# Two of the four tile turns behind the first layer moved from the matmul engine to a DMA transpose, with the work between the scan steps regrouped

## The chip, the cores and the metric

The kernel runs on one core of a Trainium2 chip. The metric is the device time of one execution in microseconds (us), lower is better. The kernel before takes 925.98 us, the median of 3 runs (925.22 to 927.23). The profile is of another, single execution of 928.0 us, in which the engines' span is 926.3 us.

## What is computed

The input x has 2 sequences of 4096 rows of 512 numbers. A state-space layer is followed by a layer that routes each row to one of 8 experts; both stand behind a normalisation and have a residual. Cut to what matters:

```python
def attn(x):                      # x is normalised
    s = sigmoid(silu(x @ s_w1.T + s_b1) @ s_w2.T + s_b2)
    u = (x @ B_w.T + B_b) * s     # 128 states
    h[t] = h[t-1] @ A.T + u[t]    # over the 4096 steps
    y = h @ C_w.T + C_b + x @ D_w.T + D_b
    return y * sigmoid(x @ g_w.T + g_b)
def ffn(x):                       # x is normalised
    e = argmax(x @ gate_w.T)
    return x + expert_w[e] applied to x
x = x + attn(layernorm(x))
x = x + ffn(layernorm(x))
```

## The kernel before

The rows are worked off in 16 blocks of 512 rows, 256 of each sequence; a block has 4 tiles of 128 rows. All programs are written out by hand, one per engine, and each engine takes its instructions in the order written. Matmuls are done three times over in a split form (high and low part of each operand), which is why every product stands as L1382, L1383 and L1384 in a row.

In the turn of block b the matmul engine (PE, `body` at L1543) does, in this order: the state part of y of the block before (`y_state`), the two halves of the gating network s1 (L1568, L1572), the input product B into the bank "scan", and then a long stretch in which the scan of block b runs as a chain of nine small steps (`to_pairs`, `to_chunks`, `over` 0 to 5, `to_middles`; `down` gives its result back). Each step is two or three small matmuls, and VectorE (DVE) then adds them to the state z and splits it anew (L970, L972, L962, L964) before the next step can start. Between the steps PE has other work: 48 matmuls of the gate product (`gates`, bank G) and 48 of the dense product (`y_dense`, banks y0 to y3), and the tail of block b - 1.

That tail chooses the experts. When GpSimd (POOL, L569 and L572) has made the tiles of x1, the output of the first layer, PE turns each tile (`tail_turn`, four 128x128 transposes, L1466) into a PSUM bank (tiles 0 and 2 into "turned", tiles 1 and 3 into y3). ScalarE (ACT) copies it out as the high part (`tail_hi`, L680), DVE makes the low part (`tail_lo`, L1023), and eight small products per pair of tiles (`score_product`, L1482 and L1484) give the scores. `tail_back` turns the scores back (L1498) after ACT has copied them (`scoresT`, L686), DVE chooses, and `tail_ranks` counts. The eight products of the first pair stand between the eight transposes of tiles 2 and 3.

The next block's input comes another way: ACT normalises a tile (L695), splits its words into 16-bit halves (`halve`, L704), the queue of SyncE (SP) starts a DMA transpose (`flip`, L356), ACT joins the halves (`join`, L731) and copies the high part (`high`, L738), and DVE makes the low part (`low`, L1167). There are two buffers of halves, of flipped and of joined tiles. The same way is gone by one or two pieces of expert weights per block (L711, L718, L723; `halve_piece`, `join_piece`; L1155 and L1160 on DVE). `high` of tile 3 stands at the head of ACT's next body, and PE's s1 product waits for it (`xT_hi`) at the head of a block. After the 16 blocks a last phase, from about 670 us, applies the experts to the sorted rows.

## Time and profile before

| | |
|---|---|
| median of 3 runs | 925.98 us (925.22 to 927.23) |
| the profiled execution | 928.0 us, span 926.3 us |
| PE matmul busy | 904.1 us, 98% |
| PE weight load busy | 739.5 us, 80% |
| DVE busy | 704.2 us, 76% |
| ACT busy | 597.2 us, 64% |
| POOL busy | 389.8 us, 42% |
| granted clock of PE | 0.996 of full speed |

Matmuls overlap in the pipeline, so a matmul's own duration is longer than its share of the time: what counts is the distance from one start to the next. An idle time stands at an instruction with the one that released it.

### The profile page before, as it was taken

How to read it: one execution, taken by the hardware profiler on the slowest of the kernel's cores; microseconds unless marked ns; L12 is line 12 of the kernel's file. 1: busy time of each engine (PE TensorE's matmuls, PEld its weight loads, DVE VectorE, ACT ScalarE, POOL GpSimd, SP SyncE). 2: the span in 40 equal slices, each digit the busy share in tenths (PEclk: the TensorE clock that was granted, in tenths of full speed). 3: DMA queues.
4: the chain of work that ended last, by engine and by line, in shares of the span. 5: the costliest groups of instructions: out<-in, count | busy, mean ns of one | idle time of the engine just before them, and what ended most of it. 6: DMA issues, size and time to landing. Idle time of an engine off the chain costs nothing.

```text
span 926.3 us, 15829 instructions
## 1 busy us (share of the span) xinstructions
PE 904.1 (98%) x4565; PEld 739.5 (80%) x4566; DVE 704.2 (76%) x1725; ACT 597.2 (64%) x826; POOL 389.8 (42%) x492
## 2 busy tenths in 40 slices
PE   8999999999999999999999999999999999999995
PEld 7777888888888888888888888888868887888884
DVE  6778979788888979788888979788787465555552
ACT  5568676857767675867767685857534345666661
POOL 1032536181634536181634527181623453333432
PEclk9999999999999999999999999999999999999998
DMA  8435384746657474748557485846789868999881
GB/s 311 131 91 140 89 206 114 205 108 171 151 140 187 89 198 120 204 111 171 153 137 186 90 199 118 206 113 178 254 275 413 336 234 243 224 218 219 192 187 39
DMA packets 203593, 165.55 MB, mean 179 GB/s; under 512 B 128245, under 2 KB 161781, under 8 KB 202496
## 3 DMA queue, kind: packets, MB, share of 16 engines
q1 hardware_dynamic: 192576, 130.89, 55.6%
q0 software_dynamic: 10800, 33.70, 10.7%
q8 instruction: 36, 0.59, 0.3%
q14 instruction: 37, 0.30, 0.1%
q10 hardware_dynamic: 144, 0.07, 0.0%
HBM read 81.63 MB, written 54.68 MB: 147 GB/s over the span
## 4 chain that ended last, share of the span: by engine, by line
PE 88%; DVE 3%; issue 2%; SPq 1%; ACT 1%; DMA 1%; POOL 0%; ACTq 0%; DVEq 0%; POOLq 0%
PE y L1662 19%; PE y L1382 7%; PE y L1383 7%; PE y L1384 7%; PE gates L1382 7%; PE gates L1384 6%; PE gates L1383 6%; PE scan L1527 3%; PE turned L1568 3%; PE gates L1568 3%; PE scan L1382 2%; PE scan L1383 2%; PE scan L1384 2%; PE turned L1650 2%; PE scores L1484 2%
## 5 line engine op out<-in xcount | busy, mean ns | idle before, releaser
L1662 PE MATMUL y<-experts,x1T_hi 128*128 x568 | 180.7, 399 | 2.6 <-issue 2.5
L578 POOL TENSOR_SCALAR ln_var_eps<-ln_mean_var 128x4 f32<-128x4 f32 x16 | 3.6, 224 | 302.3 <-DVE ln_mean_var L1017 302.2
L1662 PEld LDWEIGHTS y<-experts,x1T_hi 128*128 128x128 f32 x568 | 103.4, 188 | 24.1 <-issue 4.2
L623 POOL DMA_INDIRECT out<-gate,ids x71 | 72.0, 1015 | 111.1 <-DVE gate L1347 68.2
L1662 PE MATMUL y<-experts,x1T_lo 128*128 x284 | 111.4, 392 | 0.0
L1347 DVE TENSOR_TENSOR gate<-y,raw_weights 128x512 f32<-128x512 f32 x71 | 49.1, 691 | 75.6 <-PE y L1662 50.4
L1382 PE MATMUL gates<-GwT_hi,xT_hi 128*128 128x512 f32 x256 | 104.6, 409 | 0.0
L1382 PE MATMUL y<-DwT_hi,xT_hi 128*128 128x512 f32 x256 | 101.8, 398 | 0.5 <-DVE gateT L939 0.5
L731 ACT ACTIVATE joined<-flipped 128x1024 uint16<-128x1024 uint16 x60 | 82.3, 1371 | 29.7 <-DVE xT_lo L1167 21.1
L1383 PE MATMUL y<-DwT_lo,xT_hi 128*128 128x512 f32 x256 | 100.3, 392 | 0.0
L1384 PE MATMUL y<-DwT_hi,xT_lo 128*128 128x512 f32 x256 | 100.3, 392 | 0.0
L1384 PE MATMUL gates<-GwT_hi,xT_lo 128*128 128x512 f32 x256 | 100.2, 392 | 0.0
L1383 PE MATMUL gates<-GwT_lo,xT_hi 128*128 128x512 f32 x256 | 100.2, 391 | 0.0
L572 POOL TENSOR_TENSOR x_rows<-x_rows,y_biased 128x512 f32<-128x512 f32 x60 | 91.4, 1523 | 4.7
L569 POOL TENSOR_TENSOR y_biased<-y_biased,gate 128x512 f32<-128x512 f32 x60 | 79.4, 1323 | 25.5 <-DVE y_biased L1007 25.5
L970 DVE TENSOR_TENSOR z<-scan,z 128x126 f32<-128x126 f32 (+6 forms) x128 | 35.9, 280 | 54.7 <-PE scan L1527 51.1
L594 POOL DMA_INDIRECT routed_rows<-x_rows,dest x64 | 64.3, 1004 | 24.3 <-issue 23.5
L829 ACT ACTIVATE x1T_hi<-turned 128x512 fp32r<-128x512 f32 x36 | 21.6, 599 | 70.8 <-PE turned L1650 66.5
L704 ACT ACTIVATE halves<-x_in 128x1024 uint16<-128x1024 uint16 x60 | 63.5, 1058 | 1.9
L695 ACT ACTIVATE x_in<-x_in,ln_shift,ln_rstd 128x512 f32<-128x512 f32 x60 | 48.3, 805 | 22.7 <-POOL ln_shift L562 22.7
L1662 PEld LDWEIGHTS y<-experts,x1T_lo 128*128 128x128 f32 x284 | 53.3, 188 | 11.8
L1384 PEld LDWEIGHTS gates<-GwT_hi,xT_lo 128*128 128x128 f32 x256 | 48.0, 188 | 11.1
(276 smaller groups left out, 2340.9 us busy)
## 6 DMA issues: line engine op xcount, KB each, us to landing
raw_weights<-routed_rows SPq DMA_DIRECT2D x71, 258.0 KB
x_in<-L_attn_x SPq DMA_DIRECT2D x32, 512.0 KB, 5.0
x_rows<-L_attn_x SPq DMA_DIRECT2D x32, 512.0 KB, 4.9
turned_experts<-raw_weights SPq DMA_DIRECT2D x32, 512.0 KB, 5.3
experts<-turned_experts SPq DMA_DIRECT2D x8, 2048.0 KB
raw_weights<-L_ffn_expert_w SPq DMA_DIRECT2D x32, 256.0 KB, 3.1
routed_rows<-padrow SPq DMA_DIRECT2D x9, 258.0 KB
out<-gate,ids POOLq DMA_INDIRECT x71
```

The costliest lines, as they stand in the source:

```text
L569: nc.gpsimd.tensor_tensor(yb[:, i, :], yb[:, i, :], gate[:, i, :], ALU.mult).then_inc(S_["gated"], 1)
L572: nc.gpsimd.tensor_tensor(xrow[q][:, i, 0:D], xrow[q][:, i, 0:D], yb[:, i, :], ALU.add).then_inc(S_["x1_ready"], 1)
L594: nc.gpsimd.indirect_dma_start(out=routed, out_offset=bass.IndirectOffsetOnAxis(ap=dest[q][:, i:i + 1], axis=0), in_=xrow[q][:, i, :], in_ ...
L623: nc.gpsimd.indirect_dma_start(out=out_rows, out_offset=bass.IndirectOffsetOnAxis(ap=ids[r][:, 0:1], axis=0), in_=res[r], in_offset=None, ...
L704: nc.scalar.activation(halves[n % 2][:].rearrange("p (h d) -> p h d", h=2), planes(xin[:, i, :]), ACT.Copy).then_inc(S_["x_halves"], 1)
L731: nc.scalar.activation(planes(joined[n % 2][:].rearrange("p k t -> p (k t)")), flipped[n % 2][:].rearrange("p (h k) t -> p h (k t)", h=2), ...
L1347: nc.vector.tensor_tensor(res[r], Y[m % 2][:], rows[m][:, 0:D], ALU.add).then_inc(S_["slot_result"], 1)
L1382: nc.tensor.matmul(dst, left[0], right[0], start=first, stop=False)
L1383: nc.tensor.matmul(dst, left[0], right[1], start=False, stop=False)
L1384: return nc.tensor.matmul(dst, left[1], right[0], start=False, stop=last)
L1568: nc.tensor.matmul((TP, G)[m][:], h[:, k, m * P:(m + 1) * P], xT[0][:, k, :], start=(k == 0 and h is s1T[0]), stop=False)
L1662: ins = nc.tensor.matmul(Y[m % 2][:], x2T[a][:, k, m % 2 * P:(m % 2 + 1) * P], flat[:, bass.ds(first + (w * KD + k) * D, D)], start=(k == ...
```

## The change

For tiles 2 and 3 of x1 of blocks 1 to 13, that is in the turns of blocks 2 to 14, PE's transposes are left out. ACT splits the tile into halves (`halve_x1`), SP starts a DMA transpose, ACT joins the halves (`join_x1`), and `tail_hi` and `tail_lo` read the joined tile in SBUF instead of a PSUM bank. The buffers are the four tiles of y_biased, which are free once x1 is made. In these 13 turns the order is changed too: on PE the products of the first pair stand alone, `gates` of tiles 1 and 2, `y_dense` of tile 3 and the second pair's products are regrouped, and the second `tail_back` goes behind `y_dense` of tile 3; on DVE `tail_lo`, `gate_sum(1)`, `low(b + 1, 0)`, `low_piece`, `add_identity` and `ln2_stats(3)` change places; on ACT `join(b + 1, 2)` goes behind the copies of the state. In all turns from block 1 on, ACT's gate of the old tile 3 goes behind the first sigmoid of s1.

```diff
+        def by_dma(b, i):
+
+            return 0 < b < LASTB - 1 and i >= NT // 2
+
+        def x1_on_pe(b, i):
+
+            return NT * min(b, 1) + NT // 2 * max(0, min(b, LASTB - 1) - 1) + NT * max(0, b - LASTB + 1) + i + 1
+
+        x1_halves = [yb[:, j, :].bitcast(u16) for j in range(2)]
+        x1_flipped = [yb[:, 2 + j, :].bitcast(u16).rearrange("p (c t) -> p c t", t=P) for j in range(2)]
+        x1_joined = [yb[:, j, :] for j in range(2)]
 
...
+                if by_dma(b - 1, NT - 1):
+                    for j in range(2):
+                        sp.wait_ge(S_["x1_halves"], 2 * (b - 2) + j + 1)
+                        sp.dma_start_transpose(x1_flipped[j], x1_halves[j]).then_inc(x1_turned[j], 16)
...
-                act.wait_ge(S_["x2T_psum"], NT * b + i + 1)
-
-                nc.scalar.activation(turned_rows(b, i)[0][:, :, i % 2 * P:(i % 2 + 1) * P], by_block(turn_bank(b, i)), ACT.Copy
+                if by_dma(b, i):
+                    act.wait_ge(S_["x1_joined"], 2 * (b - 1) + i - 1)
+                    src = x1_joined[i - 2].rearrange("p (k t) -> p k t", k=KD)
+                else:
+                    act.wait_ge(S_["x2T_psum"], x1_on_pe(b, i))
+                    src = by_block(turn_bank(b, i))
+                nc.scalar.activation(turned_rows(b, i)[0][:, :, i % 2 * P:(i % 2 + 1) * P], src, ACT.Copy
                                      ).then_inc(S_["x2T_hi"], 1)
+
+            def halve_x1(b, i):
+
+                act.wait_ge(S_["x1_ready"], NT * b + i + 1)
+                nc.scalar.activation(x1_halves[i - 2].rearrange("p (h d) -> p h d", h=2), planes(xrow[b % 2][:, i, 0:D]), ACT.Copy
+                                     ).then_inc(S_["x1_halves"], 1)
+
+            def join_x1(b, i):
+
+                act.wait_ge(x1_turned[i - 2], 16 * b)
+                nc.scalar.activation(planes(x1_joined[i - 2]), x1_flipped[i - 2].rearrange("p (h k) t -> p h (k t)", h=2), ACT.Copy
+                                     ).then_inc(S_["x1_joined"], 1)
 
             def scoresT(b, pair):
...
                 ahead = b < LASTB
+                dma = by_dma(b - 1, NT - 1)
                 if tail:
                     high(b, NT - 1)
-                    gates(b - 1, NT - 1)
...
+                    if tail and m == 0:
+                        gates(b - 1, NT - 1)
...
                     halve_piece(1, 1)
+                if dma:
+                    halve_x1(b - 1, 2)
+                    halve_x1(b - 1, 3)
                 if ahead:
                     halve(b + 1, 0)
                     halve(b + 1, 1)
                 else:
                     join_piece(b, 0)
                     join_piece(b, 1)
-                if tail:
+                if tail and not dma:
                     tail_hi(b - 1, 2)
                     tail_hi(b - 1, 3)
+                if tail:
                     scoresT(b - 1, 0)
-                    if ahead:
-                        join_piece(b, 0)
+                if dma:
+                    for i in range(2, NT):
+                        join_x1(b - 1, i)
+                        tail_hi(b - 1, i)
+                if tail and ahead:
+                    join_piece(b, 0)
...
-                    join(b + 1, 2)
+                    if not dma:
+                        join(b + 1, 2)
                 act.wait_ge(S_["scan_lo"], NSTEP * (b + 1))
...
                 if ahead:
+                    if dma:
+                        join(b + 1, 2)
                     high(b + 1, 2)
                     join(b + 1, 3)
...
-                nc.vector.tensor_tensor(lo, by_block(turn_bank(b, i)), hi.bitcast(f32), ALU.subtract
+                src = x1_joined[i - 2].rearrange("p (k t) -> p k t", k=KD) if by_dma(b, i) else by_block(turn_bank(b, i))
+                nc.vector.tensor_tensor(lo, src, hi.bitcast(f32), ALU.subtract
...
                 over(b, 0)
-                if tail:
+                if dma:
+                    ln2_stats(old, oldq, 3)
+                elif tail:
                     tail_lo(old, 2)
                 over(b, 1)
                 gate_sum(b, 0)
+                if dma:
+                    for j in range(2):
+                        add_identity(b + 1, j)
                 if not ahead:
                     list_tiles(0)
                 over(b, 2)
-                if tail:
+                if dma:
+                    tail_lo(old, 2)
+                elif tail:
                     tail_lo(old, 3)
-                if tail and ahead:
+                if tail and ahead and not dma:
                     for j in range(2):
                         add_identity(b + 1, j)
                 over(b, 3)
-                gate_sum(b, 1)
+                if not dma:
+                    gate_sum(b, 1)
                 over(b, 4)
-                if tail and ahead:
+                if dma:
+                    gate_sum(b, 1)
+                if tail and ahead and not dma:
                     low_piece(b, 0)
                 if not ahead:
                     list_gaps()
                     slot_experts(0, FIRST)
                 over(b, 5)
-                if ahead:
+                if dma:
+                    tail_lo(old, 3)
+                elif ahead:
                     low(b + 1, 0)
                 else:
                     slot_rows(0, FIRST)
                 to_middles(b)
+                if dma:
+                    low(b + 1, 0)
                 gate_sum(b, 2)
...
                     place(old, oldq, oldturn)
-                    ln2_stats(old, oldq, 3)
+                    if dma:
+                        low_piece(b, 0)
+                    else:
+                        ln2_stats(old, oldq, 3)
...
-                        wait(pe, S_["x2T_lo"], NT * b)
+                        wait(pe, S_["x2T_lo"], NT * (b - 1) + 2 if by_dma(b - 1, NT - 1) else NT * b)
...
                 to_chunks(b)
-                if tail:
+                if tail and not by_dma(b - 1, 2):
                     tail_turn(b - 1, 1 - q, 2, True)
+                elif tail:
+                    for n in range(KD):
+                        score_product(b - 1, 0, n)
                 gates(b, 0, 1, 2)
                 over(b, 0)
-                if tail:
+                if tail and not by_dma(b - 1, 3):
                     tail_turn(b - 1, 1 - q, 3, True)
+                elif tail:
+                    for n in range(KD, 2 * KD):
+                        score_product(b - 1, 0, n)
                 gates(b, 0, 3)
                 y_dense(b, 2, 0)
                 over(b, 1)
@@ -1615,22 +1686,38 @@
                 gates(b, 1, 0, 1)
                 if tail:
                     tail_back(b - 1, 0)
-                gates(b, 1, 2)
-                over(b, 3)
-                gates(b, 1, 3)
-                if tail:
+                if not by_dma(b - 1, NT - 1):
+                    gates(b, 1, 2)
+                    over(b, 3)
+                    gates(b, 1, 3)
+                    if tail:
+                        tail_scores(b - 1, 1)
+                    over(b, 4)
+                    y_dense(b, 3, 0, 1)
+                    if tail:
+                        tail_back(b - 1, 1)
+                    over(b, 5)
+                    gates(b, 2, 0, 1)
+                    to_middles(b)
+                    gates(b, 2, 2, 3)
+                    y_dense(b, 3, 2)
+                    down(b)
+                    y_dense(b, 3, 3)
+                else:
+                    over(b, 3)
+                    gates(b, 1, 2, 3)
+                    over(b, 4)
+                    y_dense(b, 3, 0, 1)
+                    over(b, 5)
+                    y_dense(b, 3, 2)
+                    gates(b, 2, 0)
+                    to_middles(b)
+                    gates(b, 2, 1)
                     tail_scores(b - 1, 1)
-                over(b, 4)
-                y_dense(b, 3, 0, 1)
-                if tail:
+                    gates(b, 2, 2, 3)
+                    down(b)
+                    y_dense(b, 3, 3)
                     tail_back(b - 1, 1)
-                over(b, 5)
-                gates(b, 2, 0, 1)
-                to_middles(b)
-                gates(b, 2, 2, 3)
-                y_dense(b, 3, 2)
-                down(b)
-                y_dense(b, 3, 3)
```

PE behind the step `to_chunks` in the turn of a middle block, before ("turned" is the bank, x_rows the tile of x1, x1T the turned tile, gateT the router's weights):

```order
L1527 MATMUL scan<-chunk_ends,A_powers_hi 128x256 [waits scan_lo]
L1527 MATMUL scan<-chunk_ends,A_powers_lo 128x256
L1466 MATMUL turned<-ident,x_rows 128x128 [waits x2T_lo,x1_ready]
L1484 MATMUL scores<-x1T_hi,gateT 16x256 [waits x2T_lo]
L1466 MATMUL turned<-ident,x_rows 128x128
L1484 MATMUL scores<-x1T_hi,gateT 16x256
L1466 MATMUL turned<-ident,x_rows 128x128
L1484 MATMUL scores<-x1T_hi,gateT 16x256
L1466 MATMUL turned<-ident,x_rows 128x128
L1482 MATMUL scores<-x1T_lo,gateT 8x256
L1382 MATMUL gates<-GwT_hi,xT_hi 128x512
```

and now:

```order
L1592 MATMUL scan<-chunk_ends,A_powers_hi 128x256 [waits scan_lo]
L1592 MATMUL scan<-chunk_ends,A_powers_lo 128x256
L1549 MATMUL scores<-x1T_hi,gateT 16x256 [waits x2T_lo]
L1549 MATMUL scores<-x1T_hi,gateT 16x256 x2
L1547 MATMUL scores<-x1T_lo,gateT 8x256
L1447 MATMUL gates<-GwT_hi,xT_hi 128x512
L1448 MATMUL gates<-GwT_lo,xT_hi 128x512
```

The four transposes (L1466) are gone and four score products remain between the step and the gate product; behind the next step the same holds for the other four.

ACT in the middle of a block's turn, behind the two `tail_hi` of tiles 0 and 1, before (in_ x_in is the next block's input; x1T_late is the turned tile 2 or 3; raw_weights is a piece of expert weights):

```order
L695 ACTIVATE x_in<-x_in,ln1_shift,ln1_rstd 128x512 [waits shift1_ready]
L704 ACTIVATE halves0<-x_in 128x1024 [waits x_turned_even,xn_ready]
L695 ACTIVATE x_in<-x_in,ln1_shift,ln1_rstd 128x512 [waits shift1_ready]
L704 ACTIVATE halves1<-x_in 128x1024 [waits x_turned_odd,xn_ready]
L680 ACTIVATE x1T_late_hi<-turned 128x4x128 [waits x2T_psum]
L680 ACTIVATE x1T_late_hi<-y3 128x4x128 [waits x2T_psum]
L686 ACTIVATE scoresT<-scores 16x256 [waits scoresT_psum]
L718 ACTIVATE raw_weights<-raw_weights 128x2x512 [waits expert_low0,expert_flip0]
L723 ACTIVATE raw_weights<-raw_weights 128x512 [waits expert_sent0,expert_joined0]
```

and now (y_biased holds the halves, the flipped and the joined tile of x1):

```order
L707 ACTIVATE y_biased<-x1_rows1 128x1024 [waits x1_ready] x2
L728 ACTIVATE x_in<-x_in,ln1_shift,ln1_rstd 128x512 [waits shift1_ready]
L737 ACTIVATE halves0<-x_in 128x1024 [waits x_turned_even,xn_ready]
L728 ACTIVATE x_in<-x_in,ln1_shift,ln1_rstd 128x512 [waits shift1_ready]
L737 ACTIVATE halves1<-x_in 128x1024 [waits x_turned_odd,xn_ready]
L719 ACTIVATE scoresT<-scores 16x256 [waits scoresT_psum]
L713 ACTIVATE y_biased<-y_biased 128x2x512 [waits x1_turned_third]
L701 ACTIVATE x1T_late_hi<-y_biased 128x4x128 [waits x1_joined]
L713 ACTIVATE y_biased<-y_biased 128x2x512 [waits x1_turned_fourth]
L701 ACTIVATE x1T_late_hi<-y_biased 128x4x128 [waits x1_joined]
L751 ACTIVATE raw_weights<-raw_weights 128x2x512 [waits expert_low0,expert_flip0]
L756 ACTIVATE raw_weights<-raw_weights 128x512 [waits expert_sent0,expert_joined0]
```

Two `halve_x1` (the row with x2) stand ahead of the next block's input, two `join_x1` (L713) behind the first copy of the scores.

ACT from the second copy of the scores to the end of a turn, before:

```order
L686 ACTIVATE scoresT<-scores 16x256 [waits scoresT_psum]
L690 ACTIVATE gate<-gate 128x512 [waits g_sum]
L738 ACTIVATE xT_hi<-joined1 128x4x128 [waits g_psum,joined]
L695 ACTIVATE x_in<-x_in,ln1_shift,ln1_rstd 128x512 [waits shift1_ready]
L704 ACTIVATE halves1<-x_in 128x1024 [waits x_turned_odd,xn_ready]
L731 ACTIVATE joined0<-flipped0 128x2x512 [waits xT_lo,x_turned_even]
L810 ACTIVATE hT_hi<-z_half_hi 128x128x2 [waits scan_lo]
L810 ACTIVATE hT_lo<-z_half_lo 128x128x2
L690 ACTIVATE gate<-gate 128x512 [waits g_sum]
L814 ACTIVATE hT_hi<-z 128x128x2 [waits h_sum]
L738 ACTIVATE xT_hi<-joined0 128x4x128 [waits g_psum,joined]
L731 ACTIVATE joined1<-flipped1 128x2x512 [waits xT_lo,x_turned_odd]
L738 ACTIVATE xT_hi<-joined1 128x4x128 [waits g_psum,joined]
```

and now:

```order
L719 ACTIVATE scoresT<-scores 16x256 [waits scoresT_psum]
L723 ACTIVATE gate<-gate 128x512 [waits g_sum]
L771 ACTIVATE xT_hi<-joined1 128x4x128 [waits g_psum,joined]
L728 ACTIVATE x_in<-x_in,ln1_shift,ln1_rstd 128x512 [waits shift1_ready]
L737 ACTIVATE halves1<-x_in 128x1024 [waits x_turned_odd,xn_ready]
L854 ACTIVATE hT_hi<-z_half_hi 128x128x2 [waits scan_lo]
L854 ACTIVATE hT_lo<-z_half_lo 128x128x2
L723 ACTIVATE gate<-gate 128x512 [waits g_sum]
L858 ACTIVATE hT_hi<-z 128x128x2 [waits h_sum]
L764 ACTIVATE joined0<-flipped0 128x2x512 [waits xT_lo,x_turned_even]
L771 ACTIVATE xT_hi<-joined0 128x4x128 [waits g_psum,joined]
L764 ACTIVATE joined1<-flipped1 128x2x512 [waits xT_lo,x_turned_odd]
L771 ACTIVATE xT_hi<-joined1 128x4x128 [waits g_psum,joined]
```

The join of the next block's tile 2 (joined0) went from ahead of the state's copies (hT) to behind them; the rest is as it was.

## Rows read from the trace of the kernel before

**Rows 1.** The page: busy time, share of the span and instructions of each engine

```profile
PE 904.1 (98%) x4565; PEld 739.5 (80%) x4566; DVE 704.2 (76%) x1725; ACT 597.2 (64%) x826; POOL 389.8 (42%) x492
```

**Rows 2.** Timeline of PE's weight loads: `tail_ranks` of the first and last of eight blocks

```profile
350.13 0.10 PEld L1506 LDWEIGHTS scores<-onehot,strictly_before 128*128 128x128 bf16 x1 [0.26 <-issue]
...
641.59 0.10 PEld L1506 LDWEIGHTS scores<-onehot,strictly_before 128*128 128x128 bf16 x1 [0.26 <-issue]
```

**Rows 3.** Timeline of PE, tile 2 turned: start, us, engine, line, operation

```profile
329.06 0.28 PE L1527 MATMUL scan<-chunk_ends,A_powers_hi 128*128 128x256 f32 x1
...
329.30 0.27 PE L1466 MATMUL turned<-ident,x_rows 128*128 128x128 f32 x1
...
330.21 0.39 PE L1382 MATMUL gates<-GwT_hi,xT_hi 128*128 128x512 f32 x1
```

**Rows 4.** Timeline of PE, a scan step, three gate products, the second pair's scores

```profile
339.15 0.27 PE L1527 MATMUL scan<-chunk_ends,A_powers_hi 128*128 128x224 f32 x1
...
340.06 0.51 PE L1484 MATMUL scores<-x1T_late_hi,gateT 128*16 128x256 f32 x3
...
340.99 0.25 PE L1527 MATMUL scan<-chunk_ends,A_powers_hi 128*128 128x192 f32 x1
```

**Rows 5.** Timeline of DVE, the scan steps that these two starts release

```profile
339.57 0.28 DVE L970 TENSOR_TENSOR z<-scan,z 128x112 f32<-128x112 f32 x1 [0.53 <-PE scan L1527]
...
340.45 0.28 DVE L964 TENSOR_TENSOR chunk_ends<-z,chunk_ends 128x112 fp32r<-128x112 f32 x1
...
341.39 0.27 DVE L970 TENSOR_TENSOR z<-scan,z 128x96 f32<-128x96 f32 x1
```

**Rows 6.** Timeline of DVE and PE: a step that waited for its split

```profile
326.04 0.42 DVE L964 TENSOR_TENSOR z_half_lo<-z,z_half_hi 128x256 fp32r<-128x256 f32 x1
...
326.64 0.29 PE L1382 MATMUL scan<-z_half_hi,A_powers_hi 128*128 128x256 f32 x1
```

**Rows 7.** Timeline of PE around the first `tail_back`

```profile
337.80 0.40 PE L1384 MATMUL gates<-GwT_hi,xT_lo 128*128 128x512 f32 x1
...
338.68 0.40 PE L1383 MATMUL gates<-GwT_lo,xT_hi 128*128 128x512 f32 x1
```

**Rows 8.** Timeline of PE, `down`, the state product and s1 behind it

```profile
347.03 0.28 PE L1382 MATMUL scan<-z_half_hi,A_powers_hi 128*128 128x256 f32 x1
...
351.05 0.39 PE L1382 MATMUL y<-CwT_hi,hT_hi 128*128 128x512 f32 x1
...
353.84 0.39 PE L1568 MATMUL turned<-xT_hi,s1T_hi 128*128 128x512 f32 x1
```

**Rows 9.** Timeline of ACT from the second copy of the scores to the block's end

```profile
342.35 0.35 ACT L686 ACTIVATE scoresT<-scores 16x256 f32<-16x256 f32 x1
...
344.47 1.06 ACT L704 ACTIVATE halves<-x_in 128x1024 uint16<-128x1024 uint16 x1
...
348.11 0.44 ACT L814 ACTIVATE hT_hi<-z 128x256 fp32r<-128x256 f32 x1 [0.20 <-DVE z L1258]
348.45 0.62 ACT L738 ACTIVATE xT_hi<-joined 128x512 fp32r<-128x512 f32 x1
350.36 1.38 ACT L731 ACTIVATE joined<-flipped 128x1024 uint16<-128x1024 uint16 x1 [1.29 <-DVE xT_lo L1167]
351.77 0.63 ACT L738 ACTIVATE xT_hi<-joined 128x512 fp32r<-128x512 f32 x1
```

**Rows 10.** Timeline of ACT, the same block's middle

```profile
325.50 0.59 ACT L680 ACTIVATE x1T_hi<-y 128x512 fp32r<-128x512 f32 x1
327.60 0.82 ACT L695 ACTIVATE x_in<-x_in,ln_shift,ln_rstd 128x512 f32<-128x512 f32 x1 [1.51 <-POOL ln_shift L562]
...
334.38 0.60 ACT L680 ACTIVATE x1T_late_hi<-y 128x512 fp32r<-128x512 f32 x1 [2.58 <-remote]
```

**Rows 11.** DMAs issued in 345 to 346.5 us: count, median us to landing

```profile
flipped<-halves SPq DMA_TRANSPOSE x1, 3.1
```

**Rows 12.** DMAs issued in 331 to 332 us

```profile
flipped<-halves SPq DMA_TRANSPOSE x1, 5.4
```

4 lines of the change are left out of this document (3 added, 1 removed).

## The prediction

> **What bounds the kernel now.** I read the page's busy times first: PE is busy 98% of the span, DVE 76%, ACT 64%, POOL 42% [rows 1]. Then the timeline of PE's weight loads, for the pace: the same instruction comes at 350.13 and seven blocks later at 641.59 [rows 2], so a block takes 291.46 / 7 = 41.64 us. Last the timelines of PE, DVE and ACT in one block: s1 of block b starts at 312.12 and s1 of block b + 1 at 353.84 [rows 8]; all clock times below are of this block. PE has no long wait in it. But a busy PE is not the only bound: it keeps pace with two chains that come close to it, the scan (PE, DVE, PE) and, at the block's end, ACT's way to the next block's input (`join`, `high`), without which s1 can't start. The change takes work from PE and gives work to ACT, so the question is which of these chains is late next.
>
> **What goes from PE.** Four transposes with four score products between them take 330.21 - 329.30 = 0.91 us [rows 3]; there are two such groups, 1.82 us. Eight score products alone take 340.99 - 340.06 = 0.93 us [rows 4]. So PE loses 0.89 us per block, in 13 blocks 11.6 us. All other products of PE are the same in number; only their places change.
>
> **What the regrouping costs in the scan.** A step is two products, 0.24 us, and a gate or dense product takes (340.06 - 339.15 - 0.23) / 3 = 0.228 us [rows 3, 4]. DVE starts 0.42 us after PE's step and needs 1.16 us for its four instructions (339.57 to 340.73) [rows 4, 5]; PE's next step can start 0.18 us after the end of the split (326.46 to 326.64) [rows 6]. The loop is thus 1.76 us, with slightly narrower data 1.70 and 1.65 (the last two estimated). PE's work between the steps is now: behind `to_chunks` and `over` 0, 0.24 + 0.47 + 6 x 0.228 = 2.07 us; behind `over` 1, 2.28; behind `over` 2, 2.01 with a `tail_back`, which costs 338.68 - 337.80 - 2 x 0.228 = 0.42 us [rows 7]; behind `over` 3, 4 and 5 only 0.22 + 1.37 = 1.59 us. There the loop is longer, and PE waits 0.17 + 0.11 + 0.06 = 0.34 us per block. Another DVE instruction between two steps adds nothing: from the end of a split to the next step's first addition 0.66 us pass with a gate sum between (340.73 to 341.39) [rows 5], and without one the loop itself needs 0.18 + 0.42 = 0.60.
>
> From 329.06 (`to_chunks`) on, PE's steps are then: `over` 0 at 331.13, 1 at 333.20, 2 at 335.49, 3 at 337.50, 4 at 339.26, 5 at 340.96, `to_middles` at 342.61. Behind that stand three gate products and the eight of the second pair, whose last one starts at 344.35 and ends 0.3 us later. `down` is at 342.61 + 0.24 + 0.68 + 0.93 + 1.37 = 345.83. From `down` to the state product it was 4.02 us, now 0.42 more for the second `tail_back`: 350.27. From there to s1 it is 2.79 as before [rows 8]: PE would be ready at 353.06, 0.78 before the 353.84 of now.
>
> **What ACT gets.** Two `halve_x1` have the form of the halves instruction (1.06 us, 0.97 from start to start), two `join_x1` that of the join (1.41 us to the start of the `high` that waits for it) [rows 9]. Nothing in the trace shows them with these operands; as the shapes and the memory are the same I bound each between 0.9 and 1.5 us. The first two fall into ACT's idle time: tail_hi ends at 326.09 and the next instruction waited until 327.60 [rows 10]. ACT is 0.35 late behind them (327.95). From 327.60 to the second copy of the scores at 342.35 it had 14.75 - 2.58 = 12.17 us of work [rows 9, 10]. With two joins (2.8) and some 0.4 of waiting for the first scores it comes to the second copy at 343.3. But the second pair's products now end only at 344.65, so it stands there until S = 344.7. That is where this ACT chain is fixed, with 1.4 us of slack ahead of it. The new DMA transposes have their own time hidden: issued at 327.1 and 328.4, wanted at 332.4 and 334.3. The shortest flip lands in 3.1 us [rows 11], one amid other traffic in 5.4 [rows 12]; at 5.4 both still come in time, and what is lost above it is first taken from the 1.4 us. SP's queue has each of its further flips issued later by at most the 1.3 us of two issues, and the tiles are wanted 6 us later. `tail_lo` of the last tile is wanted by PE at 343.5 and DVE makes it behind `over` 5, at 343.0: free, if narrowly.
>
> From the second copy of the scores on ACT has one serial chain: gate, high, normalise, halve, state copies, gate, state copy, join of tile 2 (moved in order, same sum), high, join of tile 3, high. Before it ran from 342.35 to 352.40, with 0.20 and 1.29 idle: 8.56 us of work [rows 9]. Now it starts at S: the last `high` ends at 344.7 + 8.56 = 353.26. s1's weight load and first product follow 0.18 later [rows 6]: 353.44. PE was ready at 353.06 and waits 0.38 us. So **ACT's chain sets the block's end**, and `gates` of the old tile 3, put behind the first sigmoid, takes idle time of ACT there and nothing else: zero.
>
> The flip of the next block's tile 3 lies inside this chain: its halves end at S + (345.53 - 342.35) = 347.88, and its join is reached at S + 8.56 - 0.63 - 1.41 = 351.22. A flip of 3.1 us lands at 351.0. The cover is only 0.2 us.
>
> **The sum.** The block takes 353.44 - 312.12 = 41.32 us against 41.64: 0.32 less, in 13 blocks 4.2 us. The profiled execution takes 928.0 us (span 926.3), so 923.8 by the sum; its time is 2.0 above the median of the runs, so I predict 925.98 - 4.2 = **921.8 us**. The last phase and blocks 0, 1 and 15 keep their time. The uncertain terms are the durations of ACT's new instructions (0.9 to 1.5 us each, in front of 1.4 us of slack: nothing, or at the long end nothing still, 4 x 0.3 = 1.2) and S itself, on which each 0.1 us is 1.3 us in all.
>
> **The rivals.** *PE keeps the bound.* If ACT's chain runs a little shorter than from the rows (0.38 us of 8.56), s1 starts at 353.06 and the block takes 40.94: 0.70 x 13 = 9.1 us, 916.9 us. If the scan waits vanish as well it is 0.89 x 13 = 11.6 us, 914.4. For it: PE is 98% busy and waits for nobody now. Against it: the chain consists of instructions whose durations vary by hundredths, and ACT starts it 2.3 us later than before. [...]
>
> *The chain eats the gain.* If S comes 0.2 to 0.4 later than worked out (PE's wait in each scan step by 0.1 longer, as with POOL's traffic beside DVE), or the chain itself is 0.3 longer, the block takes 41.6: 0 +- 0.14 x 13, 926 us.
>
> *The last flip is late: slower.* If the flip of the next tile 3 takes longer than 3.1 us, join, high and s1 all move by it. It may take 3.3; at 3.6 the gain of 0.32 is gone, and each tenth above costs 1.3 us. Half way between the two flips seen, 4.25 us, the block takes 42.28: 13 x 0.64 = 8.3 us slower, 934.3 us; at 5.4, 23 us. For it: the two added transposes push the traffic of the block's middle back, and one flip amid traffic took 5.4 [rows 12]. Against it: this flip, issued at 345.5, took 3.1 [rows 11], and nothing stands directly ahead of it in SP's queue now that did not before. The Trainium skill ("DMA: Bandwidth & Descriptors", section "Issuing engines are not separate DMA queues") says that DMAs of SP and POOL run on the same 16 engines and interleave. By that rule POOL's scatters, not only SP's queue, delay the new transposes; rows 12 agree, and it speaks for this rival.
>
> That the change doesn't do what it says is excluded by the order of the instructions: the transposes are gone from PE in 13 turns.
>
> **The numbers.** A difference below 0.2% (1.85 us) can't be told from none. ACT's chain as worked out, gain 1.9 to 6.5 us: 0.47. PE keeps the bound, 7 us and more: 0.18. The chain eats it, within 1.85 us: 0.18. The late flip or another thing on ACT, slower: 0.17. Faster 0.65, same 0.18, slower 0.17. The range that leaves out 2 in 10 goes from 915.5, above the full PE saving, to 928.5; the forecast's own is 919.5 to 924.1.
>
> **What would show it.** Right: a block of about 41.3 us in 13 blocks; before s1 PE waits some 0.4 us for `xT_hi`; ACT waits 1 us or more at the second copy of the scores and no longer for `xT_lo` ahead of the join of tile 3; waits of 0.1 to 0.2 us of PE behind `over` 3 to 5. Wrong: ACT arrives at the second copy later than the scores (new instructions too long, or the x1 flips late), ACT waits for a DMA at `join`, or PE waits at the state product for h_lo or at `tail_back`, which I count as covered by 0.2 us or more.

## The result, and the profile after

The changed kernel takes 931.6 us (931.1 to 932.5, 4 runs) against 926.0 us of the kernel before on the same chip (925.2 to 927.2): ratio 1.0061 [1.0046, 1.0076]. It is slower by 5.6 us, where the forecast had 4.2 us less. The profiled execution has a span of 930.7 us against 926.3.

The page of the kernel after, busy times, answers to [rows 1]:

```profile
PE 905.8 (97%) x4461; PEld 722.3 (78%) x4462; DVE 713.4 (77%) x1725; ACT 653.3 (70%) x878; POOL 388.2 (42%) x492
```

PE has 104 matmuls fewer and is no less busy. A busy time isn't work alone: the end of a matmul is modelled, and the first product of s1, which waited, counts 0.47 us where the ones behind it count 0.39. ACT has gained 56 us. The pace, from the timeline of the weight loads of `tail_ranks` (now L1571), answers to [rows 2]:

```profile
182.40 0.10 PEld L1571 LDWEIGHTS scores<-onehot,strictly_before 128*128 128x128 bf16 x1 [0.27 <-issue]
...
308.69 0.10 PEld L1571 LDWEIGHTS scores<-onehot,strictly_before 128*128 128x128 bf16 x1 [0.27 <-issue]
```

Three blocks take 126.29 us, so one takes 42.10 (before 41.64, forecast 41.32). The first changed block takes 41.01, the next twelve 42.1 each, but for one of 43.05. In that one ACT waits 1.13 us for the next block's first flip, which was issued at 331.94 and landed 9.8 us later.

PE at the head of a block and at the end of its scan leg; this answers to [rows 8] (s1) and [rows 6] (the first scan step):

```profile
270.56 0.47 PE L1633 MATMUL turned<-xT_hi,s1T_hi 128*128 128x512 f32 x1
...
285.86 0.39 PE L1447 MATMUL scan<-z_half_hi,A_powers_hi 128*128 128x256 f32 x1 [0.24 <-DVE z_half_lo L1010]
...
303.64 0.28 PE L1549 MATMUL scores<-x1T_late_hi,gateT 128*16 128x256 f32 x1
```

From s1 to the first scan step it is now 285.86 - 270.56 = 15.30 us; before it was 326.64 - 312.12 = 14.52. PE waits for VectorE there. From that step to the last score product it is 17.78 us.

ACT's timeline behind it, with the wait at the second copy of the scores, answers to [rows 9]:

```profile
303.95 0.37 ACT L719 ACTIVATE scoresT<-scores 16x256 f32<-16x256 f32 x1 [1.10 <-PE scores L1549]
304.24 0.61 ACT L723 ACTIVATE gate<-gate 128x512 f32<-128x512 f32 x1
...
306.11 1.06 ACT L737 ACTIVATE halves<-x_in 128x1024 uint16<-128x1024 uint16 x1
...
310.46 1.37 ACT L764 ACTIVATE joined<-flipped 128x1024 uint16<-128x1024 uint16 x1
311.86 0.63 ACT L771 ACTIVATE xT_hi<-joined 128x512 fp32r<-128x512 f32 x1
```

The chain has no gap: 303.95 to 312.49 is 8.54 us, forecast 8.56. VectorE's next `low` of tile 3 starts at 312.53, PE's s1 at 312.64.

VectorE from one `low` of tile 3 to the end of z_half_lo, kernel after:

```profile
270.45 0.69 DVE L1214 TENSOR_TENSOR xT_lo<-joined,xT_hi 128x512 fp32r<-128x512 f32 x1 [0.23 <-ACT xT_hi L771]
...
274.65 0.73 DVE L1176 SCALAR_TENSOR_TENSOR silu<-turned,s_b_col,silu 128x512 f32<-128x512 f32 x1
...
276.08 1.79 DVE L1171 TENSOR_TENSOR siluT_lo<-silu,siluT_hi 128x512 fp32r<-128x512 f32 x1
277.80 0.74 DVE L1176 SCALAR_TENSOR_TENSOR silu<-gates,s_b_col,silu 128x512 f32<-128x512 f32 x1
...
279.24 1.72 DVE L1171 TENSOR_TENSOR siluT_lo<-silu,siluT_hi 128x512 fp32r<-128x512 f32 x1
280.88 1.27 DVE L1057 BATCH_NORM_STATS2 ln_stats<-x_rows 128x6 f32<-128x512 f32 x2
...
282.35 1.68 DVE L1207 TENSOR_TENSOR raw_weights<-raw_weights 128x512 fp32r<-128x512 f32 x1
283.96 0.86 DVE L1185 SCALAR_TENSOR_TENSOR z<-scan,B_b_col,select 128x256 f32<-128x256 f32 x2
...
285.38 0.43 DVE L1010 TENSOR_TENSOR z_half_lo<-z,z_half_hi 128x256 fp32r<-128x256 f32 x1
```

The same stretch in the kernel before (it ends with [rows 6]):

```profile
311.34 0.68 DVE L1167 TENSOR_TENSOR xT_lo<-joined,xT_hi 128x512 fp32r<-128x512 f32 x1
...
315.77 0.75 DVE L1129 SCALAR_TENSOR_TENSOR silu<-turned,s_b_col,silu 128x512 f32<-128x512 f32 x1 [0.16 <-ACT silu L759]
...
317.22 1.05 DVE L1124 TENSOR_TENSOR siluT_lo<-silu,siluT_hi 128x512 fp32r<-128x512 f32 x1
318.49 0.75 DVE L1129 SCALAR_TENSOR_TENSOR silu<-gates,s_b_col,silu 128x512 f32<-128x512 f32 x1 [0.21 <-ACT silu L759]
...
319.94 1.30 DVE L1124 TENSOR_TENSOR siluT_lo<-silu,siluT_hi 128x512 fp32r<-128x512 f32 x1
321.16 1.27 DVE L1011 BATCH_NORM_STATS2 ln_stats<-x_rows 128x6 f32<-128x512 f32 x2
...
322.63 1.56 DVE L1160 TENSOR_TENSOR raw_weights<-raw_weights 128x512 fp32r<-128x512 f32 x1
324.61 0.88 DVE L1138 SCALAR_TENSOR_TENSOR z<-scan,B_b_col,select 128x256 f32<-128x256 f32 x2 [0.41 <-ACT select L775]
```

Three things are to be seen. Before, `low` of tile 3 starts 0.78 us ahead of s1; after, only 0.11, because both wait for ACT's last `high`. Before, VectorE waits for ACT in three places (0.16, 0.21, 0.41); after, it waits nowhere behind `low`, it is the late one. And the two siluT_lo have grown from 1.05 and 1.30 to 1.79 and 1.72 us. From the start of `low` to the end of z_half_lo the stretch is 15.12 us before and 15.36 after. Counted from each start to the next, the two siluT_lo add 0.45 and 0.42, the distances ahead of the first silu and behind the raw_weights row give 0.23 and 0.37 back, the rest 0.03. The way from s1 to the first scan step is then 0.67 (head start lost) + 0.24 - 0.13 = 0.78 us longer. The 0.13 is how the rows count: PE's step stands 0.05 behind z_half_lo instead of 0.18, but that product then takes 0.10 us longer.

The reason why siluT_lo grew can be read from POOL's timeline of the kernel after:

```profile
276.03 1.29 POOL L589 TENSOR_TENSOR x_rows<-x_rows,y_biased 128x512 f32<-128x512 f32 x1
277.27 1.76 POOL L586 TENSOR_TENSOR y_biased<-y_biased,gate 128x512 f32<-128x512 f32 x1
279.11 1.30 POOL L589 TENSOR_TENSOR x_rows<-x_rows,y_biased 128x512 f32<-128x512 f32 x1
280.37 1.75 POOL L586 TENSOR_TENSOR y_biased<-y_biased,gate 128x512 f32<-128x512 f32 x1
282.19 1.29 POOL L589 TENSOR_TENSOR x_rows<-x_rows,y_biased 128x512 f32<-128x512 f32 x1
```

siluT_lo starts at 276.08, just behind the start of a POOL addition that ends at 277.32, and ends at 277.87, 0.55 later. The second siluT_lo and the raw_weights row, a subtraction too, end 0.55 behind the POOL additions that end at 280.41 and 283.48. Before, siluT_lo met POOL in another phase:

```profile
316.42 1.31 POOL L569 TENSOR_TENSOR y_biased<-y_biased,gate 128x512 f32<-128x512 f32 x1
317.80 1.63 POOL L572 TENSOR_TENSOR x_rows<-x_rows,y_biased 128x512 f32<-128x512 f32 x1
```

The first of these ended at 317.73 and siluT_lo at 318.27, 0.54 behind it, but it had begun 0.8 us before siluT_lo. So these VectorE subtractions, with both inputs in SBUF, wait for the 128x512 GpSimd instruction that is in progress. The Trainium skill ("SBUF — State Buffer", section "SBUF: two separate sides") says that the two engines share a port pair as an exclusive lock, held for the whole instruction. These rows agree. One other row doesn't: `low` at 270.45 (0.69 us, two inputs in SBUF too) kept its usual length beside a 128x4 instruction of POOL that lasted from 270.12 to 271.16, so that small instruction didn't hold it up.

### The profile page after: what moved, and what is told of

It is laid out like the page before. It is cut to its first block, busy times and chain, and to the rows that moved or that the text cites. A ratio compares the mean times of both kernels' runs of the same rounds, so it can differ in the third digit from the quotient of the medians.

```text
span 930.7 us, 15673 instructions
## 1 busy us (share of the span) xinstructions
PE 905.8 (97%) x4461; PEld 722.3 (78%) x4462; DVE 713.4 (77%) x1725; ACT 653.3 (70%) x878; POOL 388.2 (42%) x492
## 4 chain that ended last, share of the span: by engine, by line
PE 58%; DVE 15%; ACT 11%; issue 7%; DMA 2%; SPq 2%; DVEq 0%; POOL 0%; ACTq 0%; POOLq 0%
PE y L1749 19%; PE gates L1447 4%; PE y L1447 4%; PE y L1449 4%; PE y L1448 4%; PE gates L1449 4%; PE gates L1448 4%; ACT joined L764 3%; PE scan L1592 3%; DVE y_biased L1053 3%; DVE siluT_lo L1171 2%; DVE ln_stats L958 2%; DVE silu L1176 2%; PE turned L1737 2%; ACT siluT_hi L799 2%
## 5 line engine op out<-in xcount | busy, mean ns | idle before, releaser
L586 POOL TENSOR_TENSOR y_biased<-y_biased,gate 128x512 f32<-128x512 f32 x60 | 90.1, 1501 | 25.5 <-DVE y_biased L1053 25.5
L589 POOL TENSOR_TENSOR x_rows<-x_rows,y_biased 128x512 f32<-128x512 f32 x60 | 79.5, 1325 | 4.7
L1449 PEld LDWEIGHTS y<-DwT_hi,xT_lo 128*128 128x128 f32 x256 | 48.0, 188 | 10.4
```

What stands on the lines that cost most here:

```text
L586: nc.gpsimd.tensor_tensor(yb[:, i, :], yb[:, i, :], gate[:, i, :], ALU.mult).then_inc(S_["gated"], 1)
L589: nc.gpsimd.tensor_tensor(xrow[q][:, i, 0:D], xrow[q][:, i, 0:D], yb[:, i, :], ALU.add).then_inc(S_["x1_ready"], 1)
L1449: return nc.tensor.matmul(dst, left[1], right[0], start=False, stop=last)
```

## The loop

A block of the kernel after, link by link: VectorE's stretch (270.45 to 285.81) 15.36, to PE's step 0.05, PE's scan leg to the last score product 17.78, to ACT's copy 0.31, ACT's chain 8.54, to the next `low` 0.04. The sum is 42.08, and the pace is 42.10. So VectorE's head stretch, PE's scan leg and ACT's tail chain follow each other in a ring, and the kernel is bound by the sum of three parts on three engines.

The first changed block is a test by itself, since the block ahead of it is still of the old form and leaves VectorE its head start (0.79 us):

```profile
102.17 0.68 DVE L1214 TENSOR_TENSOR xT_lo<-joined,xT_hi 128x512 fp32r<-128x512 f32 x1
...
108.06 1.02 DVE L1171 TENSOR_TENSOR siluT_lo<-silu,siluT_hi 128x512 fp32r<-128x512 f32 x1
```
```profile
102.96 0.39 PE L1633 MATMUL turned<-xT_hi,s1T_hi 128*128 128x512 f32 x1
...
144.20 0.47 PE L1633 MATMUL turned<-xT_hi,s1T_hi 128*128 128x512 f32 x1
```

Here siluT_lo takes 1.02 us, the first scan step comes 14.50 us behind s1, and s1 of the next block 41.24 us behind: the block that the forecast worked out (41.32). From the second changed block on `low` is only some 0.12 us ahead, the first siluT_lo takes 1.8 us, and the block 42.1.

The theory LOOP of the experiments is this ring; a microsecond taken from any part of it should show in every block, until PE's own work (40.94 us) is the longest. The experiments limit this for the first part, VectorE's, in which POOL has a say. The rivals are the DMA transposes (DMA), PE's regrouped scan leg by itself (SCAN) and, for VectorE's part, contention with POOL (PORT).

## Experiments

Each time stands beside the kernel before on the same chip (925.9 to 926.4 us). "Block" is the pace of the weight loads of `tail_ranks`.

**Two statistics taken out of VectorE's stretch.** In the changed blocks `ln2_stats(old, oldq, 0)` and `(…, 1)` go from VectorE's head stretch to behind `over` 3 and `to_middles`.

```diff
-                if tail:
+                if tail and not dma:
                     ln2_stats(old, oldq, 0)
                     ln2_stats(old, oldq, 1)
...
+                if dma:
+                    ln2_stats(old, oldq, 0)
...
                 if dma:
                     low(b + 1, 0)
+                    ln2_stats(old, oldq, 1)
```

> The changed kernel, with two of VectorE's statistics of x1 (ln2_stats 0 and 1, 0.6 us each from start to start) taken out of its stretch at the head of a block and put behind over 3 and to_middles, where VectorE waits 0.56 and 1.00 us. Theory LOOP: a block's length is the loop of VectorE's unbroken stretch from low(3) to the first split (15.36 us), the scan up to the second pair's scores (18.1) and ACT's chain to the last high (8.5), 42.1 in all. 1.2 us less in the first leg brings PE's own bound back: about 41.3 us a block, 13 x 0.76 = 9.9 us less than the changed kernel, 922 us. Theory DMA (ACT is late because the added transposes come late): no change, 931 to 932 us. Theory SCAN (the closer scan steps cost it): no change or slower, 931 to 933 us.

Measured: 926.4 us (923.5 to 928.6, 10 runs), ratio 1.0008 [0.9996, 1.0021]; block 41.6. The direction is LOOP's, and 5 us came back, fewer than expected. VectorE's timeline says why:

```profile
269.06 0.69 DVE L1214 TENSOR_TENSOR xT_lo<-joined,xT_hi 128x512 fp32r<-128x512 f32 x1 [0.23 <-ACT xT_hi L771]
...
274.69 1.79 DVE L1171 TENSOR_TENSOR siluT_lo<-silu,siluT_hi 128x512 fp32r<-128x512 f32 x1
...
282.03 0.88 DVE L1185 SCALAR_TENSOR_TENSOR z<-scan,B_b_col,select 128x256 f32<-128x256 f32 x2 [0.77 <-ACT select L810]
```

siluT_lo still meets POOL in the bad phase, and since s2 on PE waits for it, VectorE now waits 0.77 us for `select`. The stretch fell by 0.53 us to 14.83.

**ACT's chain shortened.** `halve(b + 1, 3)` (normalise and split, 1.86 us) goes ahead of the second copy of the scores, into the time in which ACT waited anyway.

```diff
+                if dma:
+                    halve(b + 1, 3)
                 if tail:
                     scoresT(b - 1, 1)
                 gates(b, 1)
                 if ahead:
                     high(b + 1, 1)
-                    halve(b + 1, 3)
+                    if not dma:
+                        halve(b + 1, 3)
```

> The changed kernel, with ACT's halve of the next block's tile 3 (normalise and halves, 1.80 us) ahead of the second copy of the scores, where ACT waits 1.14 us. Theory LOOP: ACT's leg falls by 1.1 us, a block to about 41.0 to 41.3, 917 to 921 us. Theory DMA: ACT is late at the second copy in any case, so the halve only changes places: 930 to 932 us. Theory SCAN: no change, 931 to 932 us.

Measured: 917.5 us (915.9 to 918.9), ratio 0.9907 [0.9884, 0.9929]; block 40.95 (one of 41.57). LOOP holds, and this version beats both kernels. VectorE and PE of it:

```profile
225.42 0.68 DVE L1217 TENSOR_TENSOR xT_lo<-joined,xT_hi 128x512 fp32r<-128x512 f32 x1
...
231.29 1.05 DVE L1174 TENSOR_TENSOR siluT_lo<-silu,siluT_hi 128x512 fp32r<-128x512 f32 x1
...
234.01 1.30 DVE L1174 TENSOR_TENSOR siluT_lo<-silu,siluT_hi 128x512 fp32r<-128x512 f32 x1
...
238.68 0.88 DVE L1188 SCALAR_TENSOR_TENSOR z<-scan,B_b_col,select 128x256 f32<-128x256 f32 x2 [0.42 <-ACT select L810]
```
```profile
240.70 0.29 PE L1450 MATMUL scan<-z_half_hi,A_powers_hi 128*128 128x256 f32 x1
```

`low` has its head start back, siluT_lo its 1.05 and 1.30, and from s1 (226.19) to the first scan step it is 14.51 us as before. In the one block of 41.57 `low` is only 0.44 ahead, siluT_lo takes 1.80 and 1.73 us again, and the step comes 14.97 us behind s1: the head start and the two siluT_lo change together. The other blocks take the 40.94 that the prediction gave for the rival "PE keeps the bound".

**Both.** The two edits together.

> Both edits together (statistics later, halve early). Theory LOOP: the loop is about 39.8 us and PE's own work sets the block, 40.9 to 41.1 us: 916 to 919 us, the best of all. Theories DMA and SCAN: 930 to 932 us.

Measured: 917.6 us (917.0 to 918.2), ratio 0.9909 [0.9891, 0.9927]; block 40.95. The first edit is worth 5 us while the ring binds and nothing once PE does.

**The new order alone.** All turns of x1 stay on PE; PE's new order is kept, VectorE's where it can be. Of ACT's, one part is lost, which the text put on record before the run doesn't say: `join(b + 1, 2)` depends on the same condition and stands ahead of the state copies again. The opposite, the DMA turns in PE's old order, wasn't tried: there PE wants tile 3's low part ahead of `over` 4, and VectorE makes it behind `over` 5.

```diff
         def by_dma(b, i):
-            return 0 < b < LASTB - 1 and i >= NT // 2
+            return False
...
-                if not by_dma(b - 1, NT - 1):
+                if not regrouped(b - 1):
                     gates(b, 1, 2)
```

> The new order of PE (gate, dense and score products regrouped between the scan steps, second tail_back at the end) and of VectorE as far as it can be kept, but tiles 2 and 3 turned on PE as before: no added DMA transpose and no added work on ACT. Theory LOOP: the reordering costs PE's waits behind over 3 to 5, 0.3 to 0.4 us a block, and ACT's chain has room: about 42.0 us a block, 929 to 931 us. Theory DMA: without the transposes nothing is late, as before: 926 us. Theory SCAN: all of the loss and the 0.89 us that the turns give back: 42.1 + 0.9 us a block, 940 us or more.

Measured: 955.7 us (955.3 to 956.1), ratio 1.0319 [1.0301, 1.0337]; block 43.9. That is far above the 929 to 931 us of LOOP, and of the three numbers only SCAN's "940 us or more" holds. The order costs much, and the changed kernel, with the DMA turns and the `join` moved, has most of it back. DMA as the main cause is refuted, above all by the second experiment, in which the transposes stand and the time is 917.5 us. SCAN is refuted there too, since it expected no change from ACT's move. ACT and PE:

```profile
312.15 0.37 ACT L723 ACTIVATE scoresT<-scores 16x256 f32<-16x256 f32 x1 [4.62 <-PE scores L1548]
```
```profile
318.63 0.48 PE L1446 MATMUL y<-CwT_hi,hT_hi 128*128 128x512 f32 x1 [0.68 <-DVE hT_lo L1325]
```

ACT stands 4.6 us until PE's late score products, with its whole tail chain behind it. PE then waits 0.68 us at the state product for hT_lo, the low part of the state. From the second copy of the scores (312.15) to the next s1 (321.51) 9.36 us pass, in the changed kernel 8.69. The 0.67 us are the price of the `join` at its old place, as the experiment on it below shows, in 13 blocks 8.7 of the 30 us.

**The same with ACT's chain shortened.** The edit of the second experiment on top of the order alone.

> The new order of PE and ACT with all turns of x1 kept on PE (that kernel alone took 955.7 us, 43.9 a block, with ACT standing 4.6 us at the second copy of the scores), and halve(b + 1, 3) moved ahead of the second copy of the scores. Theory (the block is a loop through ACT's chain behind the second copy of the scores): the chain gets shorter by the two halves, 1.8 to 2.1 us, as when the same move was made in the changed kernel, where it shortened the stretch from s1 to pairs as well: block 41.8 to 42.2, 928 to 933. Rival (PE's own scan leg with the turns in it sets the pace, and ACT's wait is only its slack): no change, 43.9, 954 to 957.

Measured: 936.4 us (935.8 to 938.4), ratio 1.0114 [1.0094, 1.0135]; block 42.4. The rival (no change) is refuted: 19 of the 30 us came back by ACT's move alone. The time is 3 us above what was expected. The `join` is at its old place here too, but PE no longer waits for hT_lo. s1 now follows PE's state products without a wait (313.45, then 314.15), so ACT is out of the ring and PE's own leg, with some waits for VectorE, sets the pace (three weight loads of scan steps stand idle 0.16 to 0.29 us for it). Against the second experiment, which differs in the turns, VectorE's order and the `join`, it is 42.40 - 40.95 = 1.45 us a block, more than the 0.89 that the transposes cost.

**`join` of tile 2 put back ahead of the state copies.**

```diff
                 if ahead:
                     high(b + 1, 1)
                     halve(b + 1, 3)
-                    if not dma:
-                        join(b + 1, 2)
+                    join(b + 1, 2)
```

> The changed kernel with ACT's join of the next block's tile 2 put back ahead of the copies of the state. Theory LOOP: ACT's chain keeps its sum, but hT and with it h_lo come 1.24 us later; PE waits for h_lo at the state product some 0.8 us, and s1 and the whole loop move by about 0.6: 42.7 us a block, 938 to 940 us. Rival, that only the sum of ACT's chain counts: 931 to 932 us.

Measured: 937.7 us (937.2 to 938.4), ratio 1.0127 [1.0110, 1.0145]; block 42.44. That part of the change was worth 6 us. PE shows the price of the old place:

```profile
312.01 0.48 PE L1444 MATMUL y<-CwT_hi,hT_hi 128*128 128x512 f32 x1 [0.69 <-DVE hT_lo L1322]
```

This is the path that was expected: ACT's copies of the state come later, with them hT_lo, and PE waits 0.69 us for it at the state product, in all 13 blocks. From the second copy of the scores (305.53) to s1 (314.89) 9.36 us pass instead of 8.69. Half of it comes back at the block's head, where the first scan step stands 14.96 us behind s1 instead of 15.30. The last join waits too, 0.64 us for VectorE's `low` of the tile before, but ACT's last `high` behind it ends 0.28 us ahead of s1, so that wait isn't the one that ends last.

**`gates` of the old tile 3 put back** to the head of ACT's body.

```diff
                     high(b, NT - 1)
+                    gates(b - 1, NT - 1)
...
-                    if tail and m == 0:
-                        gates(b - 1, NT - 1)
```

> The changed kernel with one edit undone: gates of the old tile 3 stand at the head of ACT's body again, ahead of the first sigmoid. The prediction priced that edit at zero, because ACT has idle time there. Loop theory (a block is VectorE's stretch from low(3) to z_half_lo, 15.4 us, then the scan leg, 17.7 us, then ACT's chain from the second copy of the scores, 8.5 us): the gates are in none of the three, since ACT is waiting for the scores 1.1 us at the end of the scan leg. Block 42.1 us, 931 to 932.5. Rival (gates delay ACT's select or its copies at the block's head, and VectorE waits for them): 0.3 us or more per block, 936 or more when put back, or 928 or less if it was the new place that hurt.

Measured: 932.9 us (931.4 to 933.3), ratio 1.0065 [1.0046, 1.0084]; block 42.1. The block is the same, as the prediction priced it.

**One statistic more in VectorE's stretch.** `ln2_stats(old, oldq, 2)` goes from behind `to_pairs` into the stretch, in the changed kernel and in the kernel before.

```diff
                     ln2_stats(old, oldq, 1)
+                    ln2_stats(old, oldq, 2)
...
                 to_pairs(b)
-                if tail:
-                    ln2_stats(old, oldq, 2)
```

> The changed kernel with a third statistic of x1 (ln2_stats 2, 0.6 us) moved from behind to_pairs into VectorE's stretch at the head of a block. Theory LOOP: VectorE has no idle time there, so each block gets its full length more, 0.6 us, in 13 blocks 7.8 us: 939 us. Rival DMA: no change, 931 to 932 us.

> The same edit on the kernel before. There VectorE has about 0.9 us of idle time in that stretch, 0.41 of it right ahead of the first split. Theory LOOP: most of the 0.6 us is absorbed, at most 0.2 us a block reach PE: 926 to 929 us, clearly less than the 7.8 us on the changed kernel. Rival (the instruction costs its length wherever it stands): 926 + 15 x 0.6 = 935 us.

Measured: changed kernel 931.9 us (931.4 to 935.0), ratio 1.0070 [1.0044, 1.0096], block 42.10, so nothing: a miss. Kernel before 927.9 us (925.6 to 931.4, 10 runs), ratio 1.0018 [1.0002, 1.0034], block 41.61, as expected; the 2 us more don't stand in the blocks. VectorE in the changed kernel with this edit:

```profile
283.00 1.87 DVE L1057 BATCH_NORM_STATS2 ln_stats<-x_rows 128x6 f32<-128x512 f32 x3
...
285.07 1.08 DVE L1207 TENSOR_TENSOR raw_weights<-raw_weights 128x512 fp32r<-128x512 f32 x1
...
287.50 0.43 DVE L1010 TENSOR_TENSOR z_half_lo<-z,z_half_hi 128x256 fp32r<-128x256 f32 x1
```

The 0.6 us more of work came out of the wait of the raw_weights row, 1.08 instead of 1.68. The stretch isn't a sum of VectorE's own work: it ends 2.32 us behind POOL's last addition (285.61 to 287.93), and in the changed kernel it is 2.33 (283.48 to 285.81).

**POOL started earlier.** `ln2_mv(old)`, which releases POOL, goes ahead of `choose` on VectorE.

```diff
+                if dma:
+                    ln2_mv(old)
                 if tail:
                     choose(old)
...
-                if tail:
+                if tail and not dma:
                     ln2_mv(old)
```

> The changed kernel with ln2_mv of the old tile moved ahead of choose on VectorE, so that POOL's rstd2 and its residual additions behind it can start earlier; VectorE's own sum of work in the stretch stays the same. Theory A (the stretch low(3) to z_half_lo ends by POOL's additions, behind each of which a two-operand instruction of VectorE ends 0.55 us later): the residual starts 0.28 us earlier (on its data instead of on rstd2), the stretch falls from 15.36 to about 15.1 or less, the block to 41.8 or less, 928 or less; if the two-operand instructions fall into another phase of POOL's, as in the kernel before (1.05 and 1.30 us instead of 1.79 and 1.72), down to 41.1, 921. Theory B (VectorE's stretch is a plain sum of its own instructions): same sum, 42.1, 931 to 932.5.

Measured: 930.7 us (929.9 to 932.9), ratio 1.0049 [1.0032, 1.0066]; block 42.0. The stretch is 15.26 us (271.03 to 286.29) and ends again 2.33 us behind POOL's last addition (283.96). POOL gained only 0.11 us against `low`, because its first product then waits for VectorE's y_biased. So theory A missed with its numbers (a block of 41.8 or less, 928 us or less), and the times can't tell 1 us from none. What speaks for it is the trace alone, the same 2.33 us behind POOL.

**POOL's product cut to an eighth.** POOL multiplies only 64 of 512 columns by the gate; the rest stays without it, so rows go to other experts.

```diff
-                    nc.gpsimd.tensor_tensor(yb[:, i, :], yb[:, i, :], gate[:, i, :], ALU.mult
+                    nc.gpsimd.tensor_tensor(yb[:, i, 0:64], yb[:, i, 0:64], gate[:, i, 0:64], ALU.mult
```

> The changed kernel with seven eighths of GpSimd's product y * gate left out (64 of 512 columns are multiplied), so that GpSimd is at work some 5 us less per block while VectorE makes siluT_lo. Theory PORT, as part of LOOP (siluT_lo takes 1.79 and 1.72 us in the changed kernel against 1.05 and 1.30 before, because GpSimd works beside it): siluT_lo falls to 0.7 to 1.1 us, VectorE's leg by 1.0 us or more, the block from 42.1 to 41.3 us or less, 920 to 922 us. Rival, that only VectorE's late start (0.7 us) and not GpSimd lengthens the leg: siluT_lo stays at 1.7 us, 931 us.

Measured: 948.8 us (947.3 to 949.4), ratio 1.0246 [1.0229, 1.0264]; blocks 42 to 44.5. As a whole it decides nothing, since something else took over. VectorE and ACT:

```profile
281.83 0.74 DVE L1171 TENSOR_TENSOR siluT_lo<-silu,siluT_hi 128x512 fp32r<-128x512 f32 x1
...
283.97 0.65 DVE L1207 TENSOR_TENSOR raw_weights<-raw_weights 128x512 fp32r<-128x512 f32 x1
```
```profile
296.24 1.38 ACT L713 ACTIVATE y_biased<-y_biased 128x1024 uint16<-128x1024 uint16 x1 [2.35 <-DMA y_biased<-y_biased]
```

For PORT it speaks plainly. The raw_weights row, with none of POOL's 128x512 instructions in progress, takes 0.65 us instead of 1.68. The second siluT_lo met only the last 0.20 us of an addition (it ends at 282.03) and takes 0.74 instead of 1.72, ending 0.54 behind it. The first siluT_lo of this block still met POOL and took 1.50. But the DMA transposes of x1 took 7.7 and 9.2 us to land, and ACT waited for them, 40.8 us in 24 of 26 joins against 2.4 us in 3 in the changed kernel. Why they are late here, by other rows scattered or by an earlier place of the scatters, stays open.

**The good edit on the kernel before.** `halve(b + 1, 3)` ahead of the second copy of the scores, in the kernel before.

> The kernel before with the one edit that made the changed kernel 14 us faster: halve(b + 1, 3) ahead of the second copy of the scores on ACT, in blocks 2 to 14. Theory (the kernel before is set by PE's own work of 41.64 us a block, and the changed kernel by the loop through ACT's chain): ACT's chain isn't what the kernel before waits for, block 41.6, within 1.5 us of the kernel before. Rival 1 (the move is good by itself, since VectorE's stretch starts earlier and PE waits less): block 41.3 or less, 922 or less. Rival 2 (the copy of the scores, now 2 us later, holds POOL's and VectorE's work behind it up): slower, 928 or more.

Measured: 936.6 us (931.5 to 941.9, 4 runs), ratio 1.0104 [1.0051, 1.0157]; blocks 41.9 to 45.1. Rival 2 was right in that it is slower by the late copy of the scores, but the one that waits is PE:

```profile
177.80 0.26 PE L1501 MATMUL scores<-ident,scoresT 16*128 16x16 f32 x2 [1.85 <-ACT scoresT L686]
...
221.34 0.27 PE L1501 MATMUL scores<-ident,scoresT 16*128 16x16 f32 x2 [1.88 <-ACT scoresT L686]
```

There `tail_back` comes early in PE's order, and the copy of the scores, now behind 1.86 us more of ACT's work, keeps PE waiting, between 0.26 and 1.89 us in each of the 13 blocks, 11.1 us in all. Another 3.1 us are two stretches at a lower clock (last section). Together that is nearly the 14.3 us that the 13 blocks of this execution take more than in the kernel before. The same edit on ACT is worth -14 us in the changed kernel and +10 us in the kernel before. What the change needed was this edit along with it.

## Why the prediction was wrong

- *Pace before 41.64 set by PE, PE loses 0.89 us a block*: right. With the ring shortened the block is 40.95, against the 40.94 of the first rival, and 917.5 us against its 916.9. All of PE's saving would have been 11.6 us; 8.5 were to be had, and only once ACT's chain was out of the way. The Trainium skill ("Perfetto Trace Analysis", section "Identifying the Most-Contended Engine") says to optimise the engine with the highest occupancy first. That is PE here, by its matmuls (98%) and its weight loads (80%); work was taken from it, and the time rose by 5.6 us.
- *Scan leg*: from the first step to the last score product 344.35 - 326.64 = 17.71 forecast, 17.78 measured. The steps behind `over` 3 to 5 take 1.74, 1.70 and 1.67 us, forecast 1.76, 1.70 and 1.65.
- *ACT's chain sets the block's end, 8.56 us behind the second copy of the scores*: right, 8.54; the new instructions took 1.06 and 1.36 us, within their bounds, and ACT's slack at the copy was 1.10 us (1.4 forecast). PE's s1 starts 0.48 us behind the product ahead of it, where 0.23 is usual, so PE waits some 0.25 us (0.38).
- *s1 to the first scan step stays 14.52 us*: **the step that failed**. The forecast took the first step (326.64) from a block of the kernel before and tied it to s1, though z_half_lo of VectorE releases it [rows 6], and VectorE's stretch hangs on ACT's last `high`. It let s1 slip to ACT's `high` without letting `low` of tile 3 slip too, and so worked out the first changed block, not those that follow. Measured 15.30: 0.67 of lost head start, 0.87 more in two siluT_lo beside POOL, less 0.76 that VectorE's former waits and the count of PE's start gave back. The 13 changed blocks take 547.5 us from s1 to s1, forecast 13 x 41.32 = 537.2. Of the 10.3 us the first block has -0.1, eleven have 0.79 each, 8.7, and the one of 43.05 has 1.7, of which its late flip is 0.95. The time measured is 9.8 us above the forecast.
- *The rival "the chain eats the gain"* let S, ACT's second copy of the scores, come 0.2 to 0.4 us late, by slower scan steps. S stands 303.95 - 270.56 = 33.39 us behind s1, forecast 32.58: 0.81 late, and by the head stretch. In the first changed block it stands 32.55 behind, on time.
- *The last flip, and the DMA transposes*: fast enough in nearly all blocks, so the rival of the late flip isn't what made the kernel slower. ACT waits for x1's transposes 2.4 us in 3 of 26 joins and for the next input's flips 3.4 us in three; 1.13 of it is in the block of 43.05. The cover is thin, as the kernel with less work on POOL shows.
- *`gates` at zero*: right. *`join` moved, "same sum"*: the sum of ACT's chain is the same, but the move was worth 6 us, because at the old place PE waits 0.69 us for hT_lo.

## What to carry to other kernels

When a forecast makes one chain late, carry its end around to the start of the next turn: every instruction that waits for the same event slips with it, and if the way leads back to the chain's start, the pace is the sum of the links and not the busiest engine. A forecast drawn from one block of the old form holds for the first block of the new one only; work out the second too. Then look for work in the ring that can go into the wait that the ring itself creates; here moving 1.9 us of ACT's work across one wait turned 5.6 us of loss into 8.5 us of gain. An edit of that kind can belong to one version of the kernel only, so test it on both.
